# Standing expert weights, casting transfers and a slot numbering on VectorE in a one-layer ViT tower with a routed FFN

## The reference

```python
logits = xf @ router_w.T
top_logits, top_idx = jax.lax.top_k(logits, K)          # K = 2
top_w = jax.nn.softmax(top_logits, axis=-1)
for e in range(E):                                       # E = 8
    w_e = jnp.sum(top_w * (top_idx == e), axis=-1)
    h = jax.nn.silu(xf @ Wg[e].T) * (xf @ Wu[e].T)       # 192 -> 768
    out = out + h @ Wd[e].T * w_e[:, None]               # 768 -> 192
return h_attn + out
```

## Time and profile before

| | before |
|---|---|
| median of 3 runs | 222.52 us (221.71 to 222.67) |
| the profiled execution, its own time | 222.33 us |
| its span, first to last instruction | 220.4 us |
| mean granted TensorE clock | 0.961 |
| busy: PE, weight loads, DVE, ACT, POOL | 87%, 66%, 68%, 61%, 60% |
| read from HBM, written | 31.65 MB, 4.36 MB |

### The profile page before, as it was taken

How to read it: one execution, slowest core, us unless ns; L and a number is a source line. 1 busy time by engine, 2 the same in 40 slices (tenths; PEclk the granted TensorE clock), 3 DMA queues, 4 the chain that set the end, 5 groups by cost and what they waited for, 6 DMA issues and landing times. The chain is left out here.

```text
span 220.4 us, 4927 instructions
## 1 busy us (share of the span) xinstructions
PE 190.8 (87%) x1575; PEld 144.4 (66%) x1589; DVE 150.8 (68%) x486; ACT 134.2 (61%) x315; POOL 131.4 (60%) x184
## 2 busy tenths in 40 slices
PE   8999969999697798699578989996999999999940
PEld 2899959999596664464154667673777666667620
DVE  1799798997983899887558977775755555555420
ACT  2654587599969698666868667564544444444430
POOL 8342399999699434869988976784222222222222
PEclk9999999999999999985969999999999999999985
DMA  5999999949852512573787777753511112222111
GB/s 154 372 398 382 355 408 408 386 162 308 240 146 49 150 52 66 149 212 100 203 281 213 239 175 189 191 123 58 118 19 18 20 19 45 42 42 45 18 21 18
DMA packets 22577, 36.34 MB, mean 165 GB/s; under 512 B 4057, under 2 KB 11545, under 8 KB 22553
## 3 DMA queue, kind: packets, MB, share of 16 engines
q1 hardware_dynamic: 19609, 33.26, 47.2%
q0 software_dynamic: 2944, 2.76, 8.6%
HBM read 31.65 MB, written 4.36 MB: 163 GB/s over the span
## 5 line engine op out<-in xcount | busy, mean ns | idle before, releaser
L1383 PE MATMUL ps<-experts 128*117 128x193 f32 (+1 forms) x320 | 54.4, 328 | 0.5 <-ACT experts L816 0.3
L1383 PEld LDWEIGHTS ps<-experts 128*117 128x117 f32 (+1 forms) x320 | 52.1, 180 | 2.0 <-DMA experts<-x_t 1.5
L430 POOL TENSOR_TENSOR experts<-stage,experts 128x528 bf16<-128x528 f32 x36 | 43.2, 1216 | 13.5 <-ACT experts L741 12.8
L1318 DVE TENSOR_TENSOR shared<-shared,ps 128x256 f32<-128x256 f32 x48 | 20.2, 421 | 36.9 <-ACT shared L925 35.3
L741 ACT CAST experts<-stage 128x528 f16<-128x528 f32 x64 | 38.8, 633 | 5.2 <-DMA stage<-w_exp 5.2
L925 ACT ACTIVATE shared<-ps 128x256 f32<-128x256 f32 x48 | 18.5, 385 | 28.4 <-PE ps L1588 26.9
L725 ACT ACTIVATE experts<-experts 128x468 f32<-128x468 f32 x39 | 21.9, 586 | 15.4 <-POOL experts L561 4.0
L685 POOL DMA_INDIRECT out<-shared x8 | 12.4, 1545 | 30.3 <-ACT shared L950 22.8
L561 POOL TENSOR_TENSOR experts<-experts 128x468 f32<-128x468 f32 x14 | 16.5, 1176 | 15.6 <-ACT experts L725 15.4
L685 POOL DMA_INDIRECT out<-shared,slot_row x8 | 14.2, 1775 | 19.4 <-ACT shared L950 16.3
L1609 PE MATMUL ps<-experts,shared 128*128 128x192 f16 (+1 forms) x96 | 23.7, 246 | 1.6 <-DVE shared L1323 1.6
(11 more groups left out here) (241 smaller groups left out, 369.7 us busy)
## 6 DMA issues: line engine op xcount, KB each, us to landing
stage<-w_exp SPq DMA_DIRECT2D x64, 264.0 KB
experts<-x_t SPq DMA_DIRECT2D x12, 472.0 KB, 8.0
experts<-x_t SPq DMA_DIRECT2D x16, 236.0 KB, 6.8
experts<-w_proj SPq DMA_DIRECT2D x8, 384.0 KB, 6.7
slot_x<-experts SPq DMA_DIRECT2D x1, 1032.0 KB, 8.0
shared<-slot_x SPq DMA_DIRECT2D x8, 129.0 KB, 3.3
out<-h SPq DMA_DIRECT2D x1, 351.0 KB
slot_x<-xs,posi POOLq DMA_INDIRECT x10
```

What stands on the lines that cost most here:

```text
L430: ops.tensor_tensor(lo_w[:, to + EW:to + EW + PW], stage[:, n % STAGES, :], hi_w[:, to:to + PW], ALU.subtract).then_inc(split_pool if on_p ...
L1318: v.tensor_tensor(hid[:, n % 2, :], act[:, n % 2, :], pcol(n % 3, BLK, BLK), ALU.mult).then_inc(hid_ready, 1)
L1383: last = mm(dst, xbuf[:, t % 2, k, 0:m], gw[:, k, :], start=k == 0, stop=k == KT - 1)
```

## The change

What it does, in the order of the kernel:

1. **Casting transfers.** The float16 parts of experts 3 to 7 are no longer cast by ACT but loaded by POOL-issued DMAs straight from the float32 weights, one per expert (`high_by_dma`). The stage pieces are still loaded for the rests, so these weights are read twice. Expert 3 is issued before rest 14 and within the squares of tile 4, experts 4 to 7 after rest 16 and after a wait for the embedding's end. A rest of expert 3 and up waits for its expert's transfer and its stage piece. ACT keeps 24 of 64 casts, all ahead of the loop.
2. **Rests.** POOL takes pieces 0 to 41 and, between its additions, 50, 53, 56, 59, 62 and 63. DVE takes the other 16, two before the loop and one in each of steps 0 to 13.
3. **Known chunks with standing weights.** For steps of chunks 0 to 7 the operands of gate_up change places: 20 matmuls of 128 columns, a 128 by 128 block of weights standing in each, the rows streaming. The result has hidden features on partitions, so turn_hidden falls away for these 24 steps, and DVE's gate writes its product to PSUM bank 4 + n mod 2.
4. **Chunks 5 to 7 through DRAM.** Only chunks 0 to 4 are gathered by picks (`STORED = 5`); 5 to 7 are still known, but loaded from `slot_x` like 8 to 15. `slot_x`, its blanking and its row numbers grow by three chunks.
5. **Slots numbered by VectorE.** 34 small operations on DVE between the second pick and the first rest, 12 of them linked (the next waits for it), put `posi`, `meta` and the shares out. POOL keeps 11 operations for the word (`expert_word`), after its last rest and before add_out(5).
6. **Scatters and additions.** After piece 41 POOL scatters 8 of 10 tiles, adds chunk 0, scatters the last 2, then add_out(1), rest 50, add_out(2), rests 53 and 56, add_out(3), rests 59 and 62, add_out(4), rest 63, the word, add_out(5) and so on. SP loads rows of chunks 5 to 8 before piece 57.

```diff
-    POOL_PIECES = 36
+    POOL_PIECES = 42
+    LATE_PIECES = (50,53,56,59,62,63)
+    STORED = 5
+    ACT_EXPERTS = 3
     def on_pool(n):
-        return n < POOL_PIECES
+        return n < POOL_PIECES or n in LATE_PIECES
+        def hid_at(n):
+
+            return pcol(4 + n % 2, 0, BLK)
         def take_rest(eng, ops, n):
-            eng.wait_ge(hi_done, n + 1)
+            if e < ACT_EXPERTS:
+                eng.wait_ge(hi_done, n + 1)
+            else:
+                eng.wait_ge(high_in[e - ACT_EXPERTS], 16)
+                eng.wait_ge(stage_in[n % STAGES], 16 * (n // STAGES + 1))
...
-            load_pieces(44, NP * E)
+            load_pieces(44, 57)
+            sp.wait_ge(scattered, 16 * 2 * TILES)
+            for c in range(STORED, STORED + 4):
+                load_rows(c)
+            load_pieces(57, NP * E)
+            for c in range(STORED + 4, CHUNKS):
+                load_rows(c)
...
+            def high_by_dma(e):
+                pool.dma_start(hi_w[:, 2 * e * EW:2 * e * EW + EW], w_exp[e, :, :]).then_inc(high_in[e - ACT_EXPERTS], 16)
             square_adds(4, 3, 4)
+            pool.wait_ge(csum_ready, 1)
+            for e in range(ACT_EXPERTS, EARLY):
+                high_by_dma(e)
             rests(14, 15)
             square_adds(4, 4, 6)
             rests(15, 16)
             square_adds(4, 6, NG)
-            rests(16, 24)
+            rests(16, 17)
+            wait_tok(pool, TILES - 1)
+            pool.wait_ge(ssq_done, TILES)
+            pool.wait_ge(blank_out, 48)
+            pool.wait_ge(vec_consts, 1)
+            for e in range(EARLY, E):
+                high_by_dma(e)
+            rests(17, 24)
...
+            pool.wait_ge(slots_ready, 1)
+            pool.wait_ge(xs_ready, 1)
+            scatter_rows(0, 4)
+            pool.wait_ge(xs_ready, 2)
+            scatter_rows(4, 8)
             pool.wait_ge(out_base, 32)
             add_out(0)
-            scatter_rows(0, 2)
+            pool.wait_ge(xs_ready, len(GROUPS))
+            scatter_rows(8, 10)
             add_out(1)
-            scatter_rows(2, 5)
+            rests(LATE_PIECES[0], LATE_PIECES[1])
             add_out(2)
-            scatter_rows(5, 8)
+            rests(LATE_PIECES[1], LATE_PIECES[3])
             add_out(3)
-            scatter_rows(8, 10)
+            rests(LATE_PIECES[3], LATE_PIECES[5])
             add_out(4)
+            rests(LATE_PIECES[5], NP * E)
+            expert_word()
...
             def hidden_high(n):
-                sc.wait_ge(hidT_done, n + 1)
-                a.copy(hh[:, n % 2], pcol(4 + n % 2, 0, BLK).rearrange("p (h t) -> p h t", h=HT)).then_inc(hh_ready, 1)
+                if n < OWN:
+                    sc.wait_ge(hid_ready, n + 1)
+                    if n >= 2:
+                        sc.wait_ge(down_step, n - 1)
+                else:
+                    sc.wait_ge(hidT_done, n - OWN + 1)
+                a.copy(hh[:, n % 2], hid_at(n).rearrange("p (h t) -> p h t", h=HT)).then_inc(hh_ready, 1)
...
-                if n >= 2:
-                    dve.wait_ge(hidT_done, n - 1)
-                v.tensor_tensor(hid[:, n % 2, :], act[:, n % 2, :], pcol(n % 3, BLK, BLK), ALU.mult).then_inc(hid_ready, 1)
+                if n >= OWN + 2:
+                    dve.wait_ge(hidT_done, n - OWN - 1)
+                elif 2 <= n < OWN:
+                    dve.wait_ge(hh_ready, n - 1)
+                    dve.wait_ge(hidT_ready, n - 1)
+                dst = hid_at(n) if n < OWN else hid[:, n % 2, :]
+                v.tensor_tensor(dst, act[:, n % 2, :], pcol(n % 3, BLK, BLK), ALU.mult).then_inc(hid_ready, 1)
...
-            rests(POOL_PIECES, POOL_PIECES + 2)
-            rest = POOL_PIECES + 2
+            mine = [n for n in range(NP * E) if not on_pool(n)]
+            rests(mine[0], mine[1] + 1)
+            done = 2
             for n in range(NSTEP):
...
-                for _ in range(2 if n < 6 else 1):
-                    if rest < NP * E:
-                        rests(rest, rest + 1)
-                        rest += 1
+                if done < len(mine):
+                    take_rest(dve, v, mine[done])
+                    done += 1
...
+                k1, k2 = 2 * BLK * r, W2 + 2 * BLK * r
+                if c < E:
+                    for j in range(2 * HT):
+                        dst = pcol(n % 3, j * P, CHUNK)
+                        mm(dst, part_w(0, off, k1 + j * P, P), x1h[:, c % 2, 0, :], start=True, stop=False)
+                        mm(dst, part_w(1, off, k1 + j * P, P), x1h[:, c % 2, 0, :], start=False, stop=False)
+                        mm(dst, part_w(0, off, k1 + j * P, P), x1l[:, c % 2, :], start=False, stop=False)
+                        mm(dst, part_w(0, off, k2 + j * P, P), x1h[:, c % 2, 1, :], start=False, stop=False)
+                        last = mm(dst, part_w(1, off, k2 + j * P, P), x1h[:, c % 2, 1, :], start=False, stop=True)
+                    last.then_inc(gu_done, 1)
+                    return
...
-                if n >= 1:
+                if n > OWN:
                     turn_hidden(n - 1)
```

More of the change, by code:

```diff
@@ L313, in vit_tower @@
         stage_in = [sem(f"stage_in{j}") for j in range(STAGES)]
+        high_in = [sem(f"high_in{j}") for j in range(ACT_EXPERTS, E)]
         hi_done = sem("hi_done")
@@ L662, in _ @@
-            link(g.tensor_copy(posi[0:TOK, :, :], posf[0:TOK, :, :]))
-            for k in range(2):
-                last = g.tensor_copy(xs[0:TOK, :, k, ROW - 1:ROW].rearrange("p t o -> p (t o)"), wsel[0:TOK, k, :])
-            link(last)
             def scatter_rows(n0, n1):
@@ L727, in high_parts @@
             def high_parts(n0, n1):
-                for n in range(n0, n1):
+                for n in range(n0, min(n1, ACT_EXPERTS * NP)):
                     e, j = divmod(n, NP)
@@ new lines, in over, with along @@
+            def over(w):
+                return spread(w.rearrange("p (o e) -> p o e", o=1), 1, TILES)
+            def along(w):
+                return spread(w.rearrange("p (t o) -> p t o", o=1), 2, E)
+            counts = pcol(6, te, E)
+            near, far = ranks[0:TOK], by_expert(beside(te))
+            total, share, second = beside(TILES), beside(TILES), beside(TILES)
+            both, slot = by_expert(beside(te)), by_expert(beside(te))
+            fulls, mores, ends = beside(E, P), beside(E, P), beside(E, P)
@@ new lines, in _ @@
+            link(v.tensor_tensor(fulls, ends, base[:, :], ALU.subtract))
+            v.tensor_scalar(meta[0:TOK, :, :, 2], wboth[0:TOK, 0], 4096.0, None, ALU.mult).then_inc(meta_ready, 1)
+            link(v.scalar_tensor_tensor(base[:, :], fulls, float(CHUNK), away[:, :], ALU.mult, ALU.add))
+            link(v.tensor_tensor(far, far, over(base[0:TOK, :]), ALU.mult))
+            link(v.tensor_tensor(slot, far, posm[0:TOK, 1], ALU.add))
+            for k in range(2):
+                last = v.tensor_tensor(posm[0:TOK, k], hot[0:TOK, k], slot, ALU.mult)
```

193 lines of the change are left out of this document (85 added, 108 removed).

## The result

The changed kernel took **235.94 us** (median of 4 runs, 234.58 to 239.24) against 222.12 for the kernel before in the same session: ratio 1.063, 95% interval 1.056 to 1.071. The profiled execution spans 232.7 us. I had forecast 220.8 with a range to 229: wrong in sign, and outside the range.

The account below looks back on a forecast made before the run. PE was taken to bound the kernel. A gain of at most 11.9 us, less 10.2 of new waits and 0.2 at the start, left 1.5 off 222.3: 220.8 us, range 218 to 223, 8 in 10 from 211 to 229.

Parts of the forecast that it names:

- PE's work: Steps 3 to 24: a step costs 1.62 us instead of 1.79, matmuls 0.056 apart; work 37.4 us, 5.4 less.
- Rival C: Gate_up in the loop: weight loads show, a matmul costs up to 0.10 us; about 228 us, chance 0.09.
- DVE's list: Before the loop: 34 small operations ahead of DVE's first rest cost 5.5 us, bounds 4.1 and 8.2.
- POOL's issues: In the front: issuing expert 3's transfer costs 1.3 us on the path, experts 4 to 7 cost 5.2 more.
- POOL then has pieces 17 to 41 ... and ends near 113: Before the loop: 25 pieces at 1.25 us plus 3 us of other work, ending near 113 instead of 109.7.
- The loop's start ... +0.2: Step 3 begins at 116.2 against 115.96, with DVE's two rests done at 113.9.
- Rival B: Shared DMA engines: transfers of experts 4 to 7 slow the stage loads; 225 to 229 us, chance 0.21.
- (a): Wait for rest 57 in step 10, its buffer freed by POOL's rest 50 behind add_out(1): 2.7 us.
- (b): Wait for rest 60 in step 12, its buffer freed by POOL's rest 53 behind add_out(2): 5.7 us.
- rival A: Late pieces load quickly, in 0.65 us, so new waits shrink or vanish: about 214 us, 210.5 without waits; chance 0.34.
- (c): Rows of chunk 9 wait for add_out(5), which stands behind the word: 1.8 us at PE's transpose.
- PE's earlier scatters are worth nothing: In the loop: scatters coming earlier count nothing in the sum, since PE bounds a step at 1.62 us.

Follow-up runs that it names:

- e4_standing: The kernel before with standing weights in chunks 0 to 7 and nothing else: 216.09 us, ratio 0.984 to the kernel before.
- e3_actcasts: The changed kernel without casting transfers (ACT casts all pieces as before) and without late pieces on POOL: 233.12 us, ratio 1.059 to the kernel before.
- e7_casting_only: The kernel before with the five casting transfers of experts 3 to 7 alone: 225.60 us, ratio 1.016 to the kernel before.
- e2_nolate: The changed kernel without late pieces on POOL, DVE taking all rests from 42 on: 224.74 us, ratio 1.023 to the kernel before.
- e10_no_scatters: The changed kernel without its ten scatters to DRAM and the wait on them: 230.15 us, ratio 1.041 to the kernel before.
- e1_spread: The changed kernel with the casting transfers of experts 4 to 7 issued one by one between POOL's pieces: 234.00 us, ratio 1.062 to the kernel before.
- e5_pool36: The changed kernel with POOL_PIECES back at 36 instead of 42: 233.01 us, ratio 1.042 to the kernel before.
- e6_gate_first: The changed kernel with no DVE rest before step 2, then two a step up to step 5: 235.03 us, ratio 1.061 to the kernel before.
- e8_no_transfers: The changed kernel without casting transfers and late pieces, all stage loads ahead of the rows, gate(0) first: 230.96 us, ratio 1.043 to the kernel before.
- e9_picks_to_7: e8_no_transfers with chunks 5 to 7 gathered by picks and the scatters between the additions again: 219.48 us, ratio 0.988 to the kernel before.

## Why the prediction was wrong, by its own steps

- **PE's work: right at the full clock.** The 20 matmuls of a gate_up stand 0.056 apart, as taken; e4_standing takes 5.6 us less from silu 3 to 24, where 21 x (1.79 - 1.62) = 3.6 were counted for it. The rest must be waits that shrank with it; they were not taken apart. Rival C fell with it, and so did the 81 ns of the Trainium skill (TensorE: Matmul & The Clock Gate, Back-to-back issue gap): the trace's rows decided. The sum had no term for the clock: at 1.2 GHz the spacing is 0.107, which cost 1.4 us of step 3 and of the `down` behind it.
- **DVE's list: 4.7 us (103.5 to 108.2) for 5.5.** It cost nothing in the end, DVE then waited 10 us for a load.
- **POOL's issues: oversized.** Expert 3's cost 0.78 and a gap of 0.33 for my 1.3; the four others 2.20 us for 5.2. The 1.3 did not reach DVE: its second pick ended at 103.5, not 104.1 + 1.3.
- **"POOL then has pieces 17 to 41 ... and ends near 113" is the step that failed.** It ended at 121.1. 25 x 1.25 took for granted that a piece is there when POOL wants it. Three things were missing. The stage loads were starved from 88 to 100 (the low parts 5 us late). Even without transfers POOL ends at 116.7, not 113 (e3_actcasts): its pieces between 77 and 99 waited for ACT's casts there, 3.81, 2.35 and 2.63 us the longest, as they had in the kernel before, so the six pieces more come on top of the old 109.7. And I drew nothing from the run's end: DVE's rests 42 and 43 need buffers that this run frees, and I priced them at 3.1 from the end of DVE's list, as if they were 36 and 37. What stood there instead is the chain above: the fifth piece of the run ends at 114.3, the load takes 3.9, and the second rest waits 2.7 more for the run's end. **"The loop's start ... +0.2" measured +9.0.**
- **Rival B named the mechanism and the sign but not the size.** It had 4 to 8 us of lost loads and 225 to 229. The loss of loads was near that, 5 us at the low parts; by itself it costs 0.4 at silu 3 and 3.9 us in the whole time, most of it behind silu 3 (e7_casting_only). At the loop's start it counted once it met POOL's long run, another 3.4, and what neither has alone. I had put both in one sum as independent terms.
- **The new waits (a) and (b): right in their chain and their sum.** Forecast 2.7 and 5.7 for pieces 57 and 60, together 8.4. Taking the late pieces out (e2_nolate) made silu 11 to 15 8.7 us shorter. PE's idle time is less, 2.28 and 2.93, with 0.90 more ahead of them; the rest is mostly step 12, which PE ran at 1.2 GHz between the two, a way to spend the time of (b) that I had not foreseen. The load's 3.6 us, kept as the only row of its kind, was a good choice, so rival A fell. (c): 0.97 us at the transpose of 181.01 for 1.8.
- **Not in any case: PE's instruction stall,** 3.9 us at step 4 (5.9 less the 2.0 of e10_no_scatters), from "PE's earlier scatters are worth nothing" (POOL's are meant). Nothing is a price that I had not bounded on the other side.
- The sum from measured terms, in PE's rows (step 24 begins at 176.99): step 3 +9.0, the stall +3.9, the other time from step 3 to 24 -1.2 (for my -3.5: 11.9 of gain less the 8.4 of (a) and (b)), and all behind step 24 +0.6 (for my +1.8): 12.3, as the spans have it. Of the 2.3 us missing in the third term 1.4 are the low clock of step 3; the other 0.9 stay open.

## What to carry to other kernels

When a change moves work between engines that share a ring of buffers, follow the ring and not the engines: who frees the buffer that the first waiting load needs, and where that stands in its engine's order. Two delays that are each hidden can't be added as zeros, for each uses up the cover of the other; try them together. And where a bundle of parts comes as one change, price each alone: here the plainest part alone is 1.6% faster, and the whole 6.3% slower. Price a wait of PE with the clock that follows it, too: two of them here were followed by three to four us at half the rate each.

## What the hardware did that I had not expected

- **A DVE operation can wait for a whole run of POOL's, not for one.** 7.15 us for an operation on 117x5 numbers and 6.10 for one on 117x192 (both in e1_spread). In the changed kernel rest 42 became ready at 118.26; POOL's pieces follow each other at 1.14 us and ended at 121.12; DVE's second rest began at 121.62. But in e3_actcasts a rest of DVE got in between two of eleven pieces (1.25 us at 112.77), as in the kernel before. What decides it isn't settled; no run was made for it.
- **An engine can run out of instructions beside scatters.** PE lost 4 to 6 us in one place, its gaps on "issue" and ACT on "remote", in the changed kernel, e5_pool36, e6_gate_first and e8_no_transfers, each time while scatters ran. It began beside stage loads at a DMA share of 0.9 to 1.0, and in the last two it went on at 0.5. It stands smaller in e7_casting_only (its rows above), and in the kernel before too, in ACT's timeline, right behind scatters at 149.3 and 150.6, at a share of only 0.42:

```profile
152.17 0.37 ACT L934 CAST shared<-ps 128x256 f16<-128x256 f32 x1 [2.42 <-remote]
```

  Without scatters it is gone (e10_no_scatters), and small where they stand between additions (e9_picks_to_7). It is no rule: e2_nolate had the eight scatters in a row at a share of 0.95 to 0.98 and no stall. That the fetch of instructions waits behind the scatters in a queue is my reading; what the runs show is that removing the scatters removed the stall and 5.8 us.
- **A casting transfer took 0.55 us of POOL to issue (2.20 for four), and the DMA engines read it at 385 GB/s, not far below the 407 of a full stretch,** but four issued together beside the stage loads left those one piece in 5 to 6 us. With the issues spread out POOL had its pieces in unbroken rows, and the kernel's time stayed (e1_spread). The Trainium skill (DMA: Bandwidth & Descriptors, Queues, rings and completion order) has the engines take turns between queues by the packet; by that rule the queue with the larger packets would get the larger part. The traces fit this: between the kernel before and e7_casting_only, queue 0 gains 720 packets and 5.41 MB, 7.5 KB each, while queue 1 has 1.7 KB in the mean. But no run varied the packet.
